# Attention by query halves over all head groups, with the first quantised layer started inside it

## The reference, cut to what matters

```python
x = x + attn(layernorm(x))     # 16 heads of 16, rotary, causal softmax, then @ Wproj
x = x + ffn(layernorm(x))      # both operands rounded to a 6-bit grid in blocks of 32, @ weight.T + bias
x = x + mamba_and_mlp(layernorm(x))   # x + mixer(rmsnorm(x)), then an MLP on rmsnorm
x = x + ffn(layernorm(x))      # the same quantised layer
# ffn's rounding, for each block of 32 values:
scales = max(max(abs(block)) / 7.5, eps);  q = nearest_on_grid(block / scales);  xd = q * scales
# attention, for each head: query i sees keys j <= i
scores = Q @ K.T / 4;  attn = softmax(where(causal, scores, lowest));  y = attn @ V
```

## Time and profile before

| | |
|---|---|
| median of 3 runs | 10458.52 us (10444.76 to 10460.83) |
| the profiled execution's own time | 10454.55 us |
| its span | 10452.9 us |
| busy | PE 76%, DVE 78%, ACT 41%, POOL 36% of the span |
| mean granted clock of TensorE | 0.893 of full speed |
| idle of PE before L1122 ended by the loop's start | 187.7 us, 15 times |

### The profile page before, as it was taken

One profiled execution on the slowest core, in us unless ns is written; L12 is line 12 of the kernel. 1 busy time (PEld: TensorE's weight loads), 2 busy tenths in 40 slices (PEclk: granted clock), 3 DMA queues, 4 the chain that ended last, 5 costly groups with the idle time before them and its releaser, 6 DMA issues. The chain is left out here.

```text
span 10452.9 us, 98748 instructions
## 1 busy us (share of the span) xinstructions
PE 7977.8 (76%) x32180; PEld 3842.6 (37%) x32180; DVE 8114.3 (78%) x12582; ACT 4258.4 (41%) x8183; POOL 3733.5 (36%) x2407
## 2 busy tenths in 40 slices
PE   5778787787867877777777778778777787787877
PEld 2343343433424334343333434324343243432434
DVE  5786968779687796877878778797787977869777
ACT  2434434254342533425335253343534434344342
POOL 1341614316143251422515235152341513416144
PEclk8898988989888898889989889898898988989889
DMA  3020020200202002020020200102011020100202
GB/s 73 1 43 8 4 46 0 49 1 8 42 0 49 1 9 42 0 49 1 15 36 0 49 1 21 30 0 50 1 30 21 0 50 1 39 11 4 46 0 49
DMA packets 248157, 229.92 MB, mean 22 GB/s; under 512 B 22918, under 2 KB 207494, under 8 KB 247446
## 3 DMA queue, kind: packets, MB, share of 16 engines
q1 hardware_dynamic: 247644, 223.49, 10.8%
HBM read 151.60 MB, written 70.25 MB: 21 GB/s over the span
## 5 line engine op out<-in xcount | busy, mean ns | idle before, releaser
L571 POOL TENSOR_TENSOR arena<-arena 128x1024 f32<-128x1024 f32 x1024 | 2410.2, 2354 | 2146.2 <-DVE arena L942 876.0
L710 ACT ACTIVATE PS<-arena,Aneg 128x512 f32<-128x512 f32 x2048 | 1413.5, 691 | 2046.8 <-DVE XNT L982 1080.6
L633 ACT ACTIVATE arena<-PS 128x512 f32<-128x512 f32 (+3 forms) x3072 | 1292.1, 508 | 887.1 <-PE PS L1145 881.1
L850 DVE TENSOR_REDUCE pm<-PS 128x1 f32<-128x512 f32 (+3 forms) x2048 | 1136.3, 583 | 440.6 <-PE PS L1125 289.5
L1242 PE MATMUL PS<-arena,sel 96*128 96x512 bf16 x2048 | 653.5, 402 | 1042.8 <-DVE arena L958 550.6
L1122 PE MATMUL PS<-arena 96*128 96x512 bf16 (+3 forms) x3072 | 1107.0, 380 | 299.8 <-PEq L1337 187.7
L543 POOL TENSOR_SCALAR_AFFINE_SELECT arena<-arena 128x512 f32<-128x512 f32 x512 | 326.3, 637 | 2251.2 <-ACT arena L633 2251.2
L1254 PE MATMUL PS<-arena,identf 128*128 128x512 f32 x2048 | 1071.4, 649 | 0.0
L1254 PE MATMUL PS<-XNT,identf 128*128 128x512 f32 x2048 | 971.8, 598 | 0.0
L1145 PE MATMUL PS<-arena 99*128 99x512 bf16 (+3 forms) x3072 | 887.5, 330 | 2.6
L1084 PE MATMUL PS<-identf,arena 128*128 128x128 f32 x1280 | 272.0, 374 | 787.4 <-POOL arena L533 673.3
(11 more groups left out here) (138 smaller groups left out, 13303.6 us busy)
## 6 DMA issues: line engine op xcount, KB each, us to landing
pieces_scratch<-arena SPq DMA_DIRECT2D x816, 64.0 KB
arena<-pieces_scratch SPq DMA_DIRECT2D x17, 1536.0 KB
arena<-in_x SPq DMA_DIRECT2D x17, 1024.0 KB, 5.5
U<-in_x SPq DMA_DIRECT2D x17, 1024.0 KB, 5.6
arena<-pieces_scratch SPq DMA_DIRECT2D x17, 1024.0 KB
arena<-pieces_scratch SPq DMA_DIRECT2D x34, 512.0 KB
out<-X SPq DMA_DIRECT2D x64, 256.0 KB, 12.3
arena<-pieces_scratch SPq DMA_DIRECT2D x34, 384.0 KB
```

Source lines behind the costliest of these rows:

```text
L571: nc.gpsimd.tensor_tensor(DB[:, n % 2], DTU[:, j, half(th)].unsqueeze(1).to_broadcast([P, SP2, TH]), BB[:, SP2 * sg:SP2 * (sg + 1), :], AL ...
L633: A(PT[s % len(PT)][:, hh, 0:w], bank(t_bank(n))[:, 0:w], ACT.Exp, scale=DH ** -0.5)\
L710: A(bank(da_bank(m)), DT[:, j, half(th)], ACT.Exp, scale=Aneg[:, j, SP2 * sg + ss:SP2 * sg + ss + 1]).then_inc(S("dA"), 1)
L850: V_.tensor_reduce(out=dst, in_=bank(u % 3)[:, 0:w], op=ALU.max, axis=AX.X, negate=True).then_inc(S("red"), 1)
```

## The change

The order of the attention is turned: `TASKS` holds (group, half) with the half outermost, so eight tasks: the first 512 queries of groups 0 to 3 (16 S and 16 T units each), then the second 512 (32 and 32 each). A task's T units start 14 units after its last S unit at the earliest (`T_AT`). The maxima are therefore turned, split and sent eight times, each for 16 rows where it was 32. `QS` is laid out half by half, and the Q stack is loaded in two halves of columns. T units keep to three banks. While the last T units run, PE turns the first two pairs of `Y` and makes the first four tiles of the projection, DVE adds them, normalises and rounds the first half, and POOL does the power and the bias for it. After the attention DVE's order is new: the second half's pairs are rounded one by one (`grid(0, [2])`, `grid(0, [3])`), with the first half's further work between them.

The core of the diff (renamed variables that follow from it are left out):

```diff
+TASKS = [(g, qc) for qc in range(NTH) for g in range(NG)]
+S_SEQ = [(k, hh, i, c) for k, (g, qc) in enumerate(TASKS) for i in range(qc * NHT, (qc + 1) * NHT)
+         for hh in range(HG) for c in range(1 + qc)]
+S_END = [sum(k <= n for k, _, _, _ in S_SEQ) for n in range(len(TASKS))]
+T_STEPS = [(k, j) for k, (g, qc) in enumerate(TASKS) for j in range((qc + 1) * TH // P)]
+T_AT = []
+for _n in range(NTU):
+    T_AT.append(max(T_AT[-1] + 1 if T_AT else 0, S_END[T_STEPS[_n // HG][0]] + LAG))
...
-        QS = view(0, 8192, BF16).rearrange("p (h t) -> p h t", h=H)
+        QS = view(0, 8192, BF16).rearrange("p (q h t) -> p q h t", q=NTH, h=H)
...
+            if f == 0:
+                at = (0, 1024, 2048, 3072, 8192)[n] + (4096 if n < 4 else 1024) * (p // 2)
+                return view(at + 512 * (p % 2), 512)
...
+        pv_at = [T_AT[HG * s + HG - 1] + 2 * HG for s in range(NST)]
+        mt_at = {S_END[k] + 2: k for k in range(len(TASKS))}
+        pieces_at = {S_END[k] + 3: k for k in range(len(TASKS))}
...
         def t_bank(n):
-            return 3 + n % 3 if n < T6 else n % 6
+            return 3 + n % 3
+        EARLY_TURN, EARLY_ROWS = NU + 1, NU + 6
+        early_row_at = {EARLY_ROWS + 2 * i: i for i in range(NHT)}
...
-            stack(sp, 0, slice(0, H), slice(0, T))
+            for qc in range(NTH):
+                stack(sp, 0, slice(0, H), half(qc))
... POOL
+            for s in range(NST):
+                if s == NST - HG:
+                    layer_power(0, 0)
+                    add_bias(0, 0)
                 if DIAG_STEP[s]:
...
-            layer_power(0, 0)
+            rescale(0, 0)
             layer_power(0, 1)
-            quantized(0, 0, 0)
-            quantized(0, 0, 1)
             layer_power(1, 0)
+            add_bias(0, 1)
+            rms_power(0, 0)
+            rescale(0, 1)
             layer_power(1, 1)
-            rms_power(0, 0)
... ACT
+                if u in (EARLY_TURN + 1, EARLY_TURN + 3):
+                    evacuate(0, [(u - EARLY_TURN) // 2])
-            evacuate(0)
-            evacuate(1)
-            squares(0, "xn", NT)
+            evacuate(0, range(NT // 4, NT // 2))
+            evacuate(1, range(NT // 4))
+            squares(0, "xn", NT, range(NT)[tiles(0)])
+            evacuate(1, range(NT // 4, NT // 2))
+            squares(0, "xn", NT, range(NT)[tiles(1)])
... DVE
+                if u in early_row_at:
+                    add_tiles(0, U, [early_row_at[u]])
+                    if u == max(early_row_at):
+                        quant_half(0, 0, 0)
-            add_tiles(0, U)
-            quant_half(0, 0, 0)
-            quant_half(0, 0, 1)
+            add_tiles(0, U, range(NHT, NT))
+            dve.wait_ge(S("xb"), 1)
+            add_tiles(1, X, range(NHT))
+            layer_norm(0, 1, lambda i: quant_rows(0, i // 2)[:, i % 2, :])
+            dve.wait_ge(S("xn"), NT)
+            grid(0, [NT // 4])
+            layer_norm(1, 0, lambda i: U[:, i, :])
+            grid(0, [NT // 4 + 1])
+            rms_rows(0, 0)
             dve.wait_ge(S("xb"), NTH)
-            add_tiles(1, X)
-            for th in range(NTH):
-                layer_norm(1, th, lambda i: U[:, i, :])
-            for th in range(NTH):
-                rms_rows(0, th)
+            add_tiles(1, X, range(NHT, NT))
+            layer_norm(1, 1, lambda i: U[:, i, :])
+            rms_rows(0, 1)
... PE
+                if u in (EARLY_TURN, EARLY_TURN + 2):
+                    pe.wait_ge(S("red"), NU)
+                    turn(0, lambda p, tt: Y[:, 2 * p + tt, :], "y", lambda p: NG, [(u - EARLY_TURN) // 2])
+                if u in early_row_at:
+                    rows(0, wproj, xt, NC, rnd=0, which=[early_row_at[u]])
-            turn(0, lambda p, tt: Y[:, 2 * p + tt, :], "y", lambda p: NTH * NG)
-            rows(0, wproj, xt, NC, rnd=0)
+            turn(0, lambda p, tt: Y[:, 2 * p + tt, :], "y", lambda p: len(TASKS), range(NT // 4, NT // 2))
+            rows(0, wproj, xt, NC, rnd=0, which=range(NHT, NT))
             quant_products(0)
```

More of the change, by code:

```diff
@@ L380, in row_bank @@
         def row_bank(stage, i):
+            if stage == 0 and i < NT // NTH:
+                return 1 + i % 2
             return i % MB if stage == 2 else i % (2 * MB)
@@ L436, in stack @@
                 n = DH * (hi - lo)
-                sp.dma_start(((QS, KS)[qk])[row:row + n, heads, cols],
+                sp.dma_start(KS[row:row + n, heads, cols] if qk else QS[row:row + n, cols.start // TH, heads, :],
                              pcd[qk, heads, lo:hi, :, cols].rearrange("h n d t -> (n d) h t"))\
@@ L844, in vector_program @@
                 if u < NU:
[L845 removed]
+                    k, g, hh, i, c, w = s_unit(u)
                     dve.wait_ge(S("S"), u + 1)
[L847 to L851 removed]
@@ new lines, in vector_program @@
+                    V_.tensor_reduce(out=(px if c else pm)[:, k % 2, hh, i % NHT:i % NHT + 1], in_=bank(u % 3)[:, 0:w],
+                                     op=ALU.max, axis=AX.X, negate=True).then_inc(S("red"), 1)
+                    if u == S_END[k] - 1 and TASKS[k][1]:
+                        dve.wait_ge(S("red"), u + 1)
+                        V_.tensor_tensor(pm[:, k % 2], pm[:, k % 2], px[:, k % 2], ALU.min).then_inc(S("pmax"), 1)
+                if u in pieces_at:
+                    k = pieces_at[u]
+                    mt = PS[0:HG * NHT, 7, 0:P]
+                    dve.wait_ge(S("mT"), k + 1)
+                    if k >= 2:
+                        dve.wait_ge(S("mrow"), 16 * PIECES * (k - 1))
+                    own.link(V_.tensor_copy(mp[:, k % 2, 0, :], mt))
+                    own.link(V_.tensor_tensor(mr[:, :], mt, mp[:, k % 2, 0, :], ALU.subtract))
+                    own.link(V_.tensor_copy(mp[:, k % 2, 1, :], mr[:, :]))
+                    V_.tensor_tensor(mp[:, k % 2, 2, :], mr[:, :], mp[:, k % 2, 1, :], ALU.subtract)\
@@ L1096, in rows @@
                         pe.wait_ge(S("v_done"), NT)
-                    banks = MB if stage == 2 else 2 * MB
+                    banks = MB if stage == 2 else 2 if stage == 0 and i < NT // NTH else 2 * MB
                     if i >= banks:
@@ L1126, in tensor_program @@
                     ins.then_inc(S("S"), 1)
-                if u >= NS1 and u % NS1 == 2 and u // NS1 <= NG:
-                    g = u // NS1 - 1
-                    pe.wait_ge(S("pmax"), g + 1)
+                if u in mt_at:
+                    k = mt_at[u]
+                    if TASKS[k][1]:
+                        pe.wait_ge(S("pmax"), sum(qc for _, qc in TASKS[:k + 1]))
+                    else:
+                        pe.wait_ge(S("red"), S_END[k])
                     if turned:
```

157 lines of the change are left out of this document (70 added, 87 removed).

## The result

The changed kernel takes 10408.03 us (median of 5 runs, 10398.61 to 10417.66); the kernel before, run beside it, 10456.75. The ratio is 0.9956 [0.9941, 0.9971]: a gain of 48.7 us, where 139 were forecast. The sign was right and the time lies in the range of 10255 to 10440 us, but two thirds of the gain are missing. The profiled execution took 10398.61 us, with a span of 10397.0; it is the shortest of the five.

What follows compares the result with a forecast made beforehand. PE bounds the attention's two-kind stretches, DVE the S-only ones and the middle's chain. Middle gains 11.0 us, attention loses 2.3: 8.7 an iteration, 139 in 16, so 10320 us; range 10255 to 10440.

Steps and rivals of the forecast that it cites:

- the borders' rival: Attention: PE and DVE wait for each other at the borders; 10440 to 10475 us; chance 14 in 100.
- the three banks in T-only: End of attention, T units alone: less running ahead of ACT with three banks costs 0.8 us (none to 3).
- PE's early work: T-only stretch: two pairs turned and four projection tiles on PE add 4.5 us to the path.
- POOL under DVE's rounding: T-only stretch: POOL's early power and bias fit a pause of 9 us and cost nothing.
- Two-kind stretches: Attention with S and T units together: first 36.2 us, bound above 40; second 53.3 us.
- the 3 us of climbs: Attention after the S-only stretches: two climbs of PE's clock cost 3 us, bounded by nothing and 6.
- The middle: Last `Y` to the mixer's first product: 45.8 us against 56.8, gain 11.0; bounds 43.5 and 49.
- The Q load: End of iteration: six DMAs with 1 KB rows for three with 2 KB; zero, within 2.7 us either way.
- After the middle: From the mixer's first product on (444.7 us): left as it is, but for the Q load at its end.
- the early rounding comes too late: T-only tail: DVE's work 4 us longer beside POOL; 3 to 5 us of gain lost, 10370 to 10400; 13 in 100.
- the half-clock rival: Starts of both two-kind stretches: PE's clock stays low, iteration 6.3 us longer, 10560 us; 7 in 100.

Runs made afterwards that it cites:

- the fastest kernel: Changed kernel with six banks for the last 32 T units, the last four steps' corners masked by PE, two late pairs rounded together: 10337.22 us.

## Why the prediction was wrong

It forecast 8.7 us an iteration and got 3.4. That the time still lies in the range is not the mechanism's merit: the forecast's own bounds ended at 10400, and only the part added for the borders' rival, up to 10440, takes in 10408. The lower bound doesn't follow from its terms either: a middle of 43.5 us and an attention 3 us shorter than forecast give 10235 us, not 10270. By its own steps:

**The step that failed: the three banks in T-only.** "With three banks instead of six T units can run ahead of ACT by less while PE makes a V product of 1.0 us: estimated 0.8 us (none to 3)." Measured alone, without early work, it is 4.2 us an iteration (24.8 against 20.6), outside its bounds; six banks with PE's masks give back 2.3 in the changed kernel. The rows to work it out were there: in the earlier trace rows ACT needs about 2 us for a step's four exponentials, and by the earlier trace rows PE needs 0.86 for four T units and 1.0 for a V product. Six banks let PE run a step ahead; with three, PE stops at the fourth T unit, and the V product behind it delays the next three. That is a loss in each full step, not once. The other terms of the stretch were right: 20.5 us with six banks and no early work was forecast, 20.6 measured; 4.5 for PE's early work, 4.7 measured. That 20.6, 4.2 and 4.7 make up the 29.5 is no test of its own, as each is a difference of these kernels.

**What it took for free and was not: POOL under DVE's rounding.** "Nothing" holds within 0.2 us in the changed kernel, where the banks hide it (the experiment with late rounding has 29.3 us). But it is why six banks alone bring nothing there. The place was only costed for POOL's own added work.

**Two-kind stretches.** From the first T unit to the last S unit 102.7 us were measured and 101.6 forecast (36.2 + 9.1 + 53.3 + 3), so the sum was near, with parts off in both directions: the first stretch and the gap 3.5 over, the second 2.4 under once the 3 us of climbs are counted with it. The clock cost less than was put down for it. In the changed kernel it fell to its lower level in the gap in nine iterations of 16, and holding it up took 1.4 us off, 2.1 in the fastest kernel. The first climb was not tested by an edit; behind it the clock is low for 0.9 us, where it was 1.8 before. The trace read here was a favourable one: in the seven other kernels that leave the second stretch as it is, it takes 54.2 to 55.0 us. The first stretch came towards its upper bound, and DVE binds there, as the borders' rival said; that rival's 57 us for the second and its total did not come.

**The middle.** 45.8 forecast, 46.0 measured. The gain is 1.0 us smaller than forecast, 0.8 of it since the iteration that was read had a longer middle (56.8) than the mean (56.0). In the other direction the same choice took 142.8 for an attention of 143.0.

**The Q load.** Forecast was zero, within 2.7 us either way; measured is a gain of 0.9 us in the changed kernel, 1.2 alone. That is some 15 us of the 49 and goes with the number of DMAs, which the step counted only as issues on SP.

**After the middle.** Of this stretch the prediction says that "the change leaves as it is". But 0.8 us were lost there before the load. The granted clock is low for longer behind the mixer's first product (3.1 for 1.8 us of the 15 behind it, by means). The loss goes with the shorter middle: up to the load the seven other kernels with a middle of 43 to 47 us take 403.0 to 403.4 us, the four with the middle of before 402.1 to 402.8. That the clock is the cause was not tested.

Together: banks 3.4 us over their term, the rest of the attention 0.8, the middle 1.0, what follows it 0.9, less 0.9 of the load: 5.2 us of the 5.3 missing (8.7 less 3.4). The rival "the early rounding comes too late" did not come about; the half-clock rival had the place but not the price.

## What to carry to other kernels

An engine that fills buffers for another, and has a long operation between short ones, needs enough buffers to cover it: count, per step, how far it can run ahead, and charge the shortfall in every step. When a limit is lifted and nothing comes back, look for a second one under it in the same stretch before giving the edit up; here six banks were worth nothing alone and, with PE's masks, some 30 us more than the change as made. And read the value that a term starts from as a mean over iterations, not from one.

## What the runs showed of the hardware

POOL's corner (128x512, in place) takes 0.64 us. In each of the 16 iterations of the changed kernel one took 3.16 to 3.17 us, and with six banks 4.34 to 4.35. The list of the line's instructions, with their shortest, median and longest in ns, in the changed kernel:

```profile
L569 POOL TENSOR_SCALAR_AFFINE_SELECT arena<-arena x512: 627/634/3169, 167.3 to 9901.7; 128x512 f32<-128x512 f32 x171
```

The timelines of POOL and of DVE in the changed kernel's fourth iteration, where the long one begins at 2213.03:

```profile
2213.03 4.34 POOL L569 TENSOR_SCALAR_AFFINE_SELECT arena<-arena 128x512 f32<-128x512 f32 x3 [6.34 <-ACT arena L661]
2218.55 0.63 POOL L569 TENSOR_SCALAR_AFFINE_SELECT arena<-arena 128x512 f32<-128x512 f32 x1 [1.18 <-ACT arena L661]
```

```profile
2212.00 1.28 DVE L265 SCALAR_TENSOR_TENSOR arena<-arena 128x512 f32<-128x512 f32 x2
2213.21 1.28 DVE L267 SCALAR_TENSOR_TENSOR arena<-arena 128x512 f32<-128x512 f32 x2
2214.41 1.28 DVE L271 TENSOR_TENSOR arena<-arena 128x512 f32<-128x512 f32 x2
2215.61 0.25 DVE L903 RECIPROCAL rl<-PS 128x16 f32<-128x16 f32 x1
```

The long corner lasts from 2213.03 to 2216.20. All that time DVE rounds, by operations with two tensor operands in SBUF back to back, which keep their 0.64 each; the corner ends 0.5 us after the last of them (2215.69). The Trainium skill ("SBUF — State Buffer", section "SBUF: two separate sides") calls the pair of ports that DVE and GpSimd share an exclusive lock for the whole instruction; this agrees, and the trace adds that POOL did not get in between DVE's operations, which came one after another. It can go the other way too. DVE's L251 took 1.69 us for 0.17 in the third iteration, and ended with POOL's addition of the bias:

```profile
1596.30 1.69 DVE L251 TENSOR_SCALAR sc<-am 128x16 f32<-128x16 f32 x1
```

```profile
1595.63 2.34 POOL L549 TENSOR_TENSOR X<-X,bias 128x1024 f32<-128x1024 f32 x1
```

In a stretch where all DMA engines are full, the loads that hold the 3.1 MB of Q (36.9 us) took 1.2 to 1.8 us less with Q as six DMAs than as three.
